# Expert biases of two chunks added in one go, from row tiles, behind the first experts of even chunks

## What is computed

```
x = x + conv_attention(layernorm_over_channels(x))   # instance norm, q/k/v, softmax in 8x8 windows, projection
t = tokens(x)                                        # one token per pixel, 32 channels
n = layernorm(t)
p = softmax(n @ router_w + router_b)                 # 8 experts
top_p, top_i = top_k(p, 2);  top_p = top_p / sum(top_p)
t = t + sum over the 2 chosen e of top_p[e] * (n @ expert_w[e] + expert_b[e])
```

## Time and profile before

| | us |
|---|---|
| median of 3 runs | 388.28 |
| lowest and highest | 387.21, 388.77 |
| the profiled execution | 385.65 |
| its span in the profile | 383.7 |
| PE, DVE, ACT, POOL busy in it | 350.6, 323.6, 274.9, 165.8 |

### The profile page before, as it was taken

How to read it: one execution, slowest core, us unless ns; L and a number is a source line. 1 busy time by engine, 2 the same in 40 slices (tenths; PEclk the granted TensorE clock), 3 DMA queues, 4 the chain that set the end, 5 groups by cost and what they waited for, 6 DMA issues and landing times.

```text
span 383.7 us, 12597 instructions
## 1 busy us (share of the span) xinstructions
PE 350.6 (91%) x5318; PEld 185.8 (48%) x5318; DVE 323.6 (84%) x419; ACT 274.9 (72%) x477; POOL 165.8 (43%) x193
## 2 busy tenths in 40 slices
PE   4999899999999969999999999989898798797995
PEld 2556466666666636566565655655522122121221
DVE  0599899998998879998998978999976997996773
ACT  3668678778778868787688798766467588584743
POOL 8510001221221220668534202378586648859652
PEclk9999999999999999999999999999999999898999
DMA  7700000310000000000000100013312454544542
GB/s 297 326 3 3 3 3 2 78 37 3 3 3 3 3 2 2 3 2 3 2 2 22 39 2 2 3 32 82 84 27 62 123 146 134 157 113 135 151 140 109
DMA packets 12871, 22.50 MB, mean 59 GB/s; under 512 B 2960, under 2 KB 5136, under 8 KB 12432
## 3 DMA queue, kind: packets, MB, share of 16 engines
q1 hardware_dynamic: 12240, 19.93, 17.9%
q10 hardware_dynamic: 576, 1.77, 1.2%
HBM read 5.96 MB, written 4.19 MB: 26 GB/s over the span
## 4 chain that ended last, share of the span: by engine, by line
PE 58%; DVE 18%; ACT 7%; issue 5%; SPq 5%; DMA 3%; POOL 2%; POOLq 0%; ACTq 0%; DVEq 0%
PE psum L629 14%; PE psum L648 9%; PE psum L614 7%; PE psum L656 4%; SPq L285 4%; PE psum L586 3%; PE psum L454 3%; PE psum L578 3%; PE psum L598 3%; PE psum L559 3%; DVE neg_max L1218 3%; DVE window_work L1221 2%; PE psum L788 2%; DMA weights_sb<-weights 2%; DVE window_work L1363 2%
## 5 line engine op out<-in xcount | busy, mean ns | idle before, releaser
L337 POOL TENSOR_TENSOR o_norm<-o_tok,o_rden 128x128 f32<-128x128 f32 x64 | 25.4, 417 | 167.7 <-DVE o_rden L1231 167.7
L930 ACT ACTIVATE probs<-psum 128x512 f32<-128x512 f32 x128 | 74.6, 594 | 17.8 <-PE psum L629 15.7
L629 PE MATMUL psum<-weights_sb,window_work 128*128 128x128 f32 x512 | 81.6, 281 | 5.9 <-DVE window_work L1221 3.4
L1221 DVE TENSOR_TENSOR window_work<-psum,neg_max 128x1024 f32<-128x1024 f32 x64 | 78.4, 1225 | 2.2
L629 PEld LDWEIGHTS psum<-weights_sb,window_work 128*128 128x128 f32 x512 | 57.4, 140 | 47.2 <-issue 27.3
L1218 DVE TENSOR_REDUCE neg_max<-psum 128x16 f32<-128x1024 f32 x64 | 76.7, 1198 | 1.6 <-PE psum L614 1.6
L648 PE MATMUL psum<-probs,v_cols 128*32 128x64 f32 x2048 | 54.8, 225 | 0.4 <-DVE o_tok L1229 0.2
L648 PEld LDWEIGHTS psum<-probs,v_cols 128*32 128x32 f32 x2048 | 34.8, 109 | 28.2 <-issue 24.8
L913 ACT ACTIVATE stage<-k_sb,weights_sb 128x512 f32<-128x512 f32 x64 | 44.1, 720 | 0.0
L1229 DVE STREAM_TRANSPOSE o_tok<-psum 128x512 f32<-128x512 f32 x32 | 22.9, 716 | 19.2 <-PE psum L648 19.1
L614 PE MATMUL psum<-stage 32*64 32x256 f32 x1024 | 35.8, 387 | 1.5 <-DVE window_work L1221 0.8
(11 more groups left out here) (134 smaller groups left out, 609.0 us busy)
## 6 DMA issues: line engine op xcount, KB each, us to landing
stage<-act_all SPq DMA_DIRECT2D x144, 64.0 KB, 2.0
out<-out_sb SPq DMA_DIRECT2D x16, 256.0 KB, 2.3
stage<-in_x SPq DMA_DIRECT2D x3, 1024.0 KB, 11.5
gate_rows<-gate_parts SPq DMA_DIRECT2D x16, 128.0 KB, 2.6
weights_sb<-weights ACTq DMA_DIRECT2D x1, 811.5 KB, 15.2
stage<-in_x SPq DMA_DIRECT2D x1, 768.0 KB, 5.1
gate_f<-gate_sel ACTq DMA_DIRECT2D x1, 512.0 KB, 11.2
weights_sb<-weights ACTq DMA_DIRECT2D x1, 320.0 KB, 7.9
```

The lines of the kernel that those rows point to most:

```text
L629: last = nc.tensor.transpose(bank[TURN_BANKS[v % 2]][:, b * P:b * P + P], heads.rearrange("p h k -> p (h k)"), const["c_ident"][:, :])
L930: nc.scalar.activation(probs[:, w % 4, :], bank[TURN_BANKS[w % 2]][:, :], ACT.Exp).then_inc(exp_done, 1)
L1221: nc.vector.tensor_tensor(shifted_unit[:, unit % 2, :, :, :], t, m_t.unsqueeze(3).to_broadcast([P, IMG, HEADS, TOK]), ALU.add).then_inc(sh ...
```

## The change

From chunk 2 on, the biases are no longer added one by one. Each even chunk c adds its own and that of chunk c + 1 behind its first experts: two products of 32 rows each, from the rows of `c_eb` and of the gates that belong to the chunk, into banks 6 and 7. Chunks c and c + 1 have their rows side by side (rows 0 to 31 and 32 to 63, or 64 to 95 and 96 to 127), so they are different row tiles of the array. Before the two products PE waits until the bank of c + 1 is preset (`preset` at c). The first experts of each chunk now wait for the preset of their own bank. Chunks 0 and 1 keep a bias over all 128 rows in their first half.

```diff
--- before.py
+++ after.py
@@ -200,7 +200,6 @@
         EARLY = 2
         REP_FIRST = 2
         PRESET_FIRST = 2
-        NORM_CHUNKS = 6
 
         def slot(c):
 
@@ -792,17 +791,23 @@
 
             def bias(c):
 
-                if c < PRESET_FIRST:
-                    wait_past(pe, summed, c - 1)
-                else:
-                    pe.wait_ge(preset, c + 1 - PRESET_FIRST)
+                wait_past(pe, summed, c - 1)
                 if c == 1:
                     pe.wait_ge(x2_done, CHUNKS + X2)
+                pe.wait_ge(gate_step[0], GATE_OPS + ONE)
+                nc.tensor.matmul(bank[6 + c % 2][:, :], const["c_eb"][:, c % QUAD, :], gate_f32[:, 0:CHUNK],
+                                 start=True, stop=False, skip_group_check=True)
+
+            def bias_pair(c):
+
                 quad = c // QUAD
+                pe.wait_ge(preset, c + 2 - PRESET_FIRST)
                 pe.wait_ge(gate_step[quad], GATE_OPS + ONE)
-                nc.tensor.matmul(bank[6 + c % 2][:, :], const["c_eb"][:, c % QUAD, :],
-                                 gate_f32[:, quad % 2 * CHUNK:(quad % 2 + 1) * CHUNK],
-                                 start=(c < PRESET_FIRST), stop=False, skip_group_check=True)
+                for m in (c, c + 1):
+                    rows = slice(m % QUAD * 32, m % QUAD * 32 + 32)
+                    nc.tensor.matmul(bank[6 + m % 2][:, :], const["c_eb"][rows, m % QUAD, :],
+                                     gate_f32[rows, quad % 2 * CHUNK:(quad % 2 + 1) * CHUNK],
+                                     start=False, stop=False, skip_group_check=True)
 
             def side(c, eh):
 
@@ -847,15 +852,17 @@
                     gate_pair(c, eh, 1)
                     side(c, eh)
                     if eh == 1:
-                        if c >= NORM_CHUNKS:
-                            bias(c)
+                        if c >= PRESET_FIRST:
+                            pe.wait_ge(preset, c + 1 - PRESET_FIRST)
                         experts(c, 0)
+                        if c >= PRESET_FIRST and c % 2 == 0:
+                            bias_pair(c)
                         if c == 0:
                             project(CHUNKS - 1, at=TURN_BANKS[1])
                     else:
                         if c >= 1:
                             experts(c - 1, 1)
-                        if c < NORM_CHUNKS:
+                        if c < PRESET_FIRST:
                             bias(c)
             experts(CHUNKS - 1, 1)
```

## The result

The changed kernel takes 396.82 us (median of 4, 395.14 to 397.67) against 387.89 us before: 1.0224 times the time, 95% interval 1.0189 to 1.026. The forecast was 392.4, 389.0 to 394.8: slower, as it said, but by 8.9 us where it said 4.1, and outside its range.

A forecast was written before the change was run, and what follows sets the result against it. SP's issuing, then a chain of ACT, POOL and PE, was taken as the bound; 1.06 us at chunk 4 plus 3.1 at chunk 14 made 4.2, added to the median 388.28: 392.4 us, range 389.0 to 394.8.

The forecast's parts named there:

- SP's issuing is what the end hangs by: Expert stage's end: SP's repeats and stores, then ACT, POOL, PE, set the time; SP leaves 0.97 us.
- The pair of chunk 4: Between chunk 4's first experts and chunk 5's gates: delays DVE's chunk 5 and all behind it by 1.06 us.
- rival (b): Chunk 4's centring: emptier PE falls to half clock ahead of the pair, 1.5 us less done, 393.9 us; 13%.
- The last pair: Chunk 14: the pair waits for chunk 15's preset ahead of its gates, then half clock; 3.1 us, bounds 1.55 and 3.1.
- its own half-clock row: Second experts of chunk 9, at 350.44: eight matmuls took 1.87 us after 2.10 us of idle, against 1.00 before.
- The other pairs before the last: 0.: Pairs 2, 6, 8, 10 and 12: PE's small gain or loss is covered by DVE or SP, counted as 0.
- with a slow clock, 1 lost: Pairs 6, 8 and 10, if their cover went: 0.45 us gained each, or 1 lost at slow clock; not summed.
- one half-clock stretch: Chunk 14's end: half clock after about 2.8 us of PE idle, included in the 3.1 us term.
- Row tiles side by side, 1.06 us: Each pair's two 32-row products together take 1.06 us, as the replicate does; bounds 1.05 and 2.10.
- The rule of the matmul order: Chunk 15's gates can't pass the waiting pair on PE; if they could, the 3.1 us term would be near 0.

The follow-up runs named there:

- no_bias: The kernel before with the bias products of chunks 2 to 15 left out, all waits kept: 393.28 us, 1.0125.
- stores_act: The kernel before with output stores issued by ACT, behind the preset, instead of by SP: 386.02 us, 0.9943.
- four_single: The change, but chunks 4 and 5 get single biases at the end of their first halves, as before: 393.45 us, 1.0138.
- filler_four: The change plus one 32-row product that adds zero, where chunk 4's single bias stood: 397.13 us, 1.02.
- last_single: The change, but chunks 14 and 15 get single 128-row biases ahead of their first experts, as before: 393.63 us, 1.0128.
- stores_act_change: The change with output stores issued by ACT instead of by SP: 392.70 us, 1.0093.
- both_single: The change, but chunks 4, 5, 14 and 15 get single biases, as before; pairs only at 2, 6, 8, 10 and 12: 391.03 us, 1.0063.
- late_pair: The change with pairs moved behind the odd chunk's gates and replicate, ahead of the even chunk's second experts; chunks 14 and 15 single: 387.95 us, 0.9994.
- late_fill: late_pair plus a 32-row product adding zero in each even chunk 2 to 12, where the single bias stood: 395.34 us, 1.0207.
- late_fill_full: late_fill with the filler over all 128 rows, adding the bias of even chunks 2 to 12 twice: 388.53 us, 0.9994.

## Why the prediction came out as it did

- *SP's issuing is what the end hangs by, PE's 91% is not a bound.* Right: no_bias (14.7 us less of PE, 5 us slower) shows the second. That stores_act, with no change for PE, is 2.2 us faster shows that SP's list did hold up the end.
- *The pair of chunk 4 puts DVE's chunk 5 back, and all behind it keeps that; 1.06 us.* The mechanism was right (four_single takes it away), the size was not: 2.69 us in the profile, 3.4 in the medians. The pair is about 1.0 of it, by filler_four, where the centring ran at full clock and DVE waited 1.14 us against 0.16. The rest is a fall to half clock in the centring ahead of it, which was rival (b), at 13%, and with the right price (1.5).
- *The last pair: 3.1 us.* 3.78 in the profile, 3.2 in the medians of last_single. Wait, half clock and order of events as forecast. That PE's wait comes from the late store is shown by stores_act_change (0.41 us instead of 3.26), and the change loses 1.9 us by it, 4.1 less the 2.2 that the kernel before gains as well. PE idled 3.26 us, more than the 2.8 counted. The working also gave the second experts 1.4 us (378.60 to 380.0) where its own half-clock row has 1.87; with that it would have come to 3.6.
- *"The other pairs before the last: 0."* This is the step that failed. I costed their delay at full clock and let the cover of DVE and SP stand, and said "with a slow clock, 1 lost" without taking it into the sum. With the pair of chunk 4 and the last one undone, 2.6 us were left (both_single), and in the profile of the change 2.57 us were lost between chunks 5 and 9: 0.79 us of DVE's wait before chunk 9, behind the pair of chunk 8 at half clock, and 1.79 - 0.75 = 1.04 and 1.07 - 0.23 = 0.84 us in two DVE instructions of two SBUF operands (L1267 and L1285; 0.75 and 0.23 are what they took in the kernel before) that began just behind a POOL instruction, at 330.66 and 342.14:

```profile
330.66 1.27 POOL L393 TENSOR_TENSOR gate_f<-std_pair,std_two 128x512 f32<-128x512 f32 x1
...
342.14 1.27 POOL L422 TENSOR_TENSOR window_work<-stage,q_sb 128x512 f32<-128x512 f32 x1 [1.68 <-ACT q_sb L1053]
```

  Not all of this belongs to those pairs. In the profile of four_single the first of the two instructions takes 0.75 us again and the second still 1.09. In those of last_single and filler_four, where chunk 5 is late as with the change, the first takes 1.79. So its 1.04 us goes with the delay of chunk 5.

```profile
325.94 0.75 DVE L1278 SCALAR_TENSOR_TENSOR x_win<-std_two,weights_sb,raw_logits 128x512 f32<-128x512 f32 x1
...
336.87 1.09 DVE L1296 TENSOR_TENSOR small<-small 128x64 f32<-128x64 f32 x1
```

  The kernel before has such a long instruction too, one chunk quad earlier (L1280 at 308.49 took 1.18 us, behind a POOL instruction at 308.26). both_single, with only pairs 2, 6, 8, 10 and 12, is 2.6 us slower than before, and late_pair, with the pairs moved behind the next gates, is level: it was their place, ahead of the next gates, that cost.
- *The clock.* The prediction took one half-clock stretch from a row and no other change. In fact three terms (chunk 4, chunks 8 and 9, the end) all met half clock, since the change lowered the granted clock of the whole stage, from 0.96 and 0.92 in two profiles to 0.88. Rival (b) was one place of this and should have been the forecast. The range ended at 394.8 because it let only one more stretch in, never two. Against the 4.2 us forecast the profile has 9.2: 1.6 more at chunk 4, 2.6 between chunks 5 and 9, 0.1 up to the write-out and 0.7 at the end.
- *Row tiles side by side, 1.06 us.* Right: 1.02 for a pair against 1.98 for two full products.
- *The rule of the matmul order.* The gates didn't help anyone before the pair's end, as the rule from the Trainium skill (TensorE: Matmul & The Clock Gate, "The mechanism") had it, and the last section says what the trace's records add to it.

What stays open: which property of the products the clock goes by. late_fill against late_fill_full shows that the number and the place of the products do not decide it alone, and that their rows or their values matter. Which of the two was not tried, nor whether the change from 32-row to 128-row products and back does. All variants in which the 128-row biases were replaced by 32-row ones or left out had 0.80 to 0.88 in their profiles, and those with them or with full-row products 0.92 to 0.96, with both_single and four_single (some of either) at 0.84 and last_single at 0.82. The profiled executions are one to three for each kernel, and where a stretch falls differs between executions; the clocks of whole executions, where they are given above, are of 4 to 10 runs. That the two longer DVE instructions were held up by POOL is argued from their overlap and not tried by itself. The share of each wait in the 8.9 us is read from one profile.

## What to carry to other kernels

Before products are taken off an engine that is busy but not the bound, ask what its clock will do: work that is hidden can be what keeps the rest fast, and products of 32 rows did not stand in for products of 128 here. A grouped operation inherits the latest of its inputs' waits, and on an engine that works in order this wait is paid by everything behind it; put it behind what others wait for, and look at the last round, where no slack follows. And a queue that issues transfers back to back is a bound that no busy share shows.

## What the runs showed of the hardware

- With six fillers of 32 rows and zero weights the granted clock over 87 us was 0.80 (late_fill), with six of 128 rows and the bias as weights, in the same places and of the same columns, 0.94 (late_fill_full).
- At half clock these products took 1.8 to 2.0 times as long: eight expert products 1.94 against 1.06 us, the centring 3.78 (filler_four, at 307.36) against 1.98, a pair of row tiles 2.08 against 1.02.
- Two gate products of other rows start in the middle of a pair: at 384.07, behind the first recorded parts of the pair's two products (383.95) and ahead of their second parts (384.97). Yet DVE and ACT, which wait for these gates, start only at 386.19 and 386.10, right behind the pair's end at 386.03. Here the overlap of row tiles started work early but did not report it early. The Trainium skill (TensorE: Matmul & The Clock Gate, "The mechanism") says that starts and ends both keep the program's order. Counted by recorded parts the starts in this trace do not; for the ends the starts of the waiting engines agree with it, and the gates' own recorded end, 384.68, is a modelled one.
- A store issued by ACT took ACT's queue 0.34 us (one issued by SP took SP's 0.58):

```profile
376.91 0.34 ACTq L1061 DMA_DIRECT2D out<-out_sb  x1
```
